# A bidirectional Mamba layer and a soft mixture of experts on one core: a second softplus kept in PSUM, a reordered prologue and epilogue, experts and merges in one block

## The reference

```python
delta = softplus(delta @ dt_proj_w.T + dt_proj_b)      # dt
dA_cum = exp(reversed cumulative sum of dt * A, shifted by one position)
xs = cumsum(dt * u * B * dA_cum) / (dA_cum + 1e-12)
y = einsum('bldn,bln->bld', xs, C) + u * D             # both directions are added, then gated
```

## Time and profile before

| what | value |
|---|---|
| runs | 6036.67, 6042.24, 6041.84 us, median 6041.84 |
| span of the profiled execution | 6039.5 us (its own time is not given apart from this; the span is 2.3 us under the median) |
| busy: PE, DVE, ACT, POOL | 5055.7 (84%), 4751.8 (79%), 4091.2 (68%), 4464.2 us (74%) |
| DMA | 755.29 MB, mean 125 GB/s |
| mean granted TensorE clock | 0.925 of full speed |

### The profile page before, as it was taken

One profiled execution on the slowest core, in us unless ns is written; L12 is line 12 of the kernel. 1 busy time (PEld: TensorE's weight loads), 2 busy tenths in 40 slices (PEclk: granted clock), 3 DMA queues, 4 the chain that ended last, 5 costly groups with the idle time before them and its releaser, 6 DMA issues. The chain is left out here.

```text
span 6039.5 us, 50725 instructions
## 1 busy us (share of the span) xinstructions
PE 5055.7 (84%) x14640; PEld 2557.8 (42%) x14640; DVE 4751.8 (79%) x4049; ACT 4091.2 (68%) x6429; POOL 4464.2 (74%) x2134
## 2 busy tenths in 40 slices
PE   5888887888887878888888888888888888999988
PEld 2333333333333333333333333443333434565566
DVE  5998989998989998999999999899999871222233
ACT  3878787878887878787878887878788863111100
POOL 3999999999999999999898999998989970000000
PEclk9999899999999999999999999999999999999988
DMA  2444344444443444444443444343434432323265
GB/s 71 129 127 132 123 129 125 130 123 128 128 132 123 129 127 126 126 126 129 124 132 124 128 127 133 126 128 124 132 124 128 130 106 83 101 76 101 80 228 203
DMA packets 555572, 755.29 MB, mean 125 GB/s; under 512 B 124059, under 2 KB 272411, under 8 KB 553245
## 3 DMA queue, kind: packets, MB, share of 16 engines
q1 hardware_dynamic: 555293, 752.04, 39.8%
HBM read 662.04 MB, written 89.82 MB: 124 GB/s over the span
## 5 line engine op out<-in xcount | busy, mean ns | idle before, releaser
L628 POOL TENSOR_TENSOR g_ring<-dtu,b_ring 128x1024 f32<-128x1024 f32 x1026 | 2514.5, 2454 | 362.2 <-DVE e_ps L976 335.1
L976 DVE TENSOR_TENSOR_SCAN e_ps<-e_ps,g_ring 128x1024 f32<-128x1024 f32 x1024 | 2345.2, 2290 | 168.3 <-ACT e_ps L782 156.2
L782 ACT ACTIVATE e_ps<-dt,a_neg 128x512 f32<-128x512 f32 x2050 | 1398.5, 682 | 721.7 <-DVE v_own L998 484.6
L1141 PE MATMUL y_ps<-v_ring,ident 128*128 128x512 f32 x3088 | 1632.2, 638 | 231.9 <-DVE res_gate L959 193.8
L637 POOL TENSOR_TENSOR v_ring<-z_ring,c_ring 128x1024 f32<-128x1024 f32 x768 | 1822.2, 2373 | 0.0
L792 ACT ACTIVATE f_ring<-rsum,consts,a_neg_half 128x512 f32<-128x512 f32 x2050 | 1645.8, 803 | 0.8
L989 DVE SCALAR_TENSOR_TENSOR z_ring<-f_ring,e_ps 128x1024 f32<-128x1024 f32 x768 | 934.9, 1217 | 49.7 <-issue 1.7
L1141 PEld LDWEIGHTS y_ps<-v_ring,ident 128*128 128x128 f32 x3088 | 592.6, 206 | 884.9 <-issue 815.3
L1141 PE MATMUL y_ps<-v_own,ident 128*128 128x512 f32 x1028 | 535.4, 616 | 0.0
L1074 PE MATMUL side<-u,conv_diag 128*128 128x512 f32 x1088 | 491.8, 595 | 23.2 <-ACT disp_ring L743 18.7
L1251 ACT ACTIVATE x_act<-x_gate,x_bg 128x512 f32<-128x512 f32 x128 | 87.9, 687 | 570.8 <-PE x_gate L1283 570.8
(11 more groups left out here) (134 smaller groups left out, 5206.1 us busy)
## 6 DMA issues: line engine op xcount, KB each, us to landing
b_ring<-bc_scr SPq DMA_DIRECT2D x1027, 256.0 KB, 3.7
c_ring<-bc_scr SPq DMA_DIRECT2D x1025, 256.0 KB, 3.4
pT_scr<-rowT_ring SPq DMA_DIRECT2D x136, 256.0 KB, 4.0
m_pT<-pT_scr SPq DMA_DIRECT2D x16, 2048.0 KB, 8.7
sT_scr<-sT_ring SPq DMA_DIRECT2D x272, 64.0 KB, 2.9
x_xT<-sT_scr SPq DMA_DIRECT2D x16, 1024.0 KB, 9.2
eo_scr<-x_eo SPq DMA_DIRECT2D x32, 512.0 KB, 5.1
m_eo<-eo_scr SPq DMA_DIRECT2D x16, 1024.0 KB, 11.0
```

What stands on the lines that cost most here:

```text
L628: pool.tensor_tensor(g_ring[:, k], dtu[d][:], both(b_ring[:, k:k + 1]), ALU.mult).then_inc(g_done, 1)
L782: act.activation(e_ps[:, i % 2, h], dt[d][:, h], ACT.Exp, scale=a_neg[:, d, c, n:n + 1]).then_inc(e_done, 1)
L976: dve.tensor_tensor_scan(e, e, g, 0.0, ALU.mult, ALU.add).then_inc(scan_done, 1)
L1141: pe.matmul(y_ps[:, t % 2], ident[:], v, start=(t % (TILES // PAIRS) < 2), stop=True, skip_group_check=True).then_inc(v_used, 1)
```

## The change

Six parts; the diff is cut to what the prediction speaks of.

1. ACT applies softplus four times: both banks to SBUF (`dt_done`), then both banks in place in PSUM (`plus_done`). DVE makes the sums with two scans of 511 elements that read the PSUM banks and a row of ones in SBUF, and these scans free the banks. POOL's `cut_chunks` now waits for the banks, and ACT's `guard` for the cut.
2. `HOLD` of dt goes from 2 to 4. By `slot_tiles` this moves the second operation of three dt pairs by one tile: dt0 3 from 36 to 37, dt1 3 from 67 to 68, dt0 1 from 98 to 99 (dt1 1 stays at 6). in0 0 stays at 38, in0 1 goes from 38 to 40, slots 2 and 3 from 68 and 71 to 70 and 72, slots 4 and 5 from 100 and 102 to 102 and 104, the operations between tiles 40 and 53 by one or two.
3. Prologue: the slots' data are loaded first and waited for alone; `v_ring` and `v_own` are cleared by POOL; the order of the side operations is that of `AHEAD`; a convolution waits only for its own diagonals; the slots' transposes go through `e_ps`; the lags of different side operations are interleaved.
4. Epilogue: the same interleaving.
5. Experts and merges share one block. Five buffers of `pT`, `x1` and `rinv` are loaded while the experts run; `eo` has two buffers, filled but for the last tile during the last expert, and that tile afterwards.
6. In the merges SP issues, once the output of sequence b-1 is computed, `pT`, `x1`, `rinv` of sequence b+4, the store of b-1, and then `eo` of b+1.

```diff
-HOLD = {..., "dt0": 2, "dt1": 2, "in0": 3,
+HOLD = {..., "dt0": 4, "dt1": 4, "in0": 3,
-AHEAD = tuple((kind, i) for kind in ("in0", "conv0", "conv1") for i in range(4)) + (
-    ("x0", 0), ("x1", 0), ("dt0", 0), ("dt0", 1))
+AHEAD = tuple((kind, i) for kind in ("in0", "conv0") for i in range(4)) + (
+    ("x0", 0), ("conv1", 0), ("dt0", 0), ("dt0", 1)) + tuple(("conv1", i) for i in range(1, 4)) + (("x1", 0),)
...
+            pool.memset(v_ring[:], 0.0).then_inc(v_cleared, 1)
+            pool.memset(v_own[:], 0.0).then_inc(v_cleared, 1)
...
             def dtu_of_pair(at, s):
+                pool.wait_ge(dt_done, at.pair(s))
...
-                pool.wait_ge(rsum_done, at.pair(s))      # cut_chunks
+                for j in (s - 1, s):
+                    pool.wait_ge(side_free[at.bank(j)], at.freed(j))
...
-                        act.activation(dt[d][:, 0], side[:, at.bank(s - 1)], ACT.Softplus).then_inc(
-                            side_free[at.bank(s - 1)], 1)
-                        act.activation(dt[d][:, 1], src, ACT.Softplus).then_inc(free, 1)
+                        both_banks = (side[:, at.bank(s - 1)], src)
+                        act.activation(dt[d][:, 0], both_banks[0], ACT.Softplus)
+                        act.activation(dt[d][:, 1], both_banks[1], ACT.Softplus).then_inc(dt_done, 1)
+                        for bank in both_banks:
+                            act.activation(bank, bank, ACT.Softplus).then_inc(plus_done, 1)
...
-                        for j in (s - 1, s):
-                            dve.wait_ge(side_free[at.bank(j)], at.freed(j))
-                        sums, steps_ = halves(rsum[d]), halves(dt[d])
...
-                        dve.tensor_tensor_scan(out, data, turn, 0.0, ALU.add, ALU.mult).then_inc(rsum_done, 1)
+                        dve.memset(rsum[d][:, :, L - 1:L] if d == 0 else rsum[d][:, :, 0:1], 0.0)
+                        for h, j in enumerate((s - 1, s)):
+                            dve.wait_ge(plus_done, 2 * at.pair(s) - 1 + h)
+                            bank, sums = side[:, at.bank(j)], rsum[d][:, h]
+                            out, data = (sums[:, 0:L - 1][:, ::-1], bank[:, 1:L][:, ::-1]) if d == 0 else (
+                                sums[:, 1:L], bank[:, 0:L - 1])
+                            dve.tensor_tensor_scan(out, data, ones[:], 0.0, ALU.add, ALU.mult).then_inc(
+                                side_free[at.bank(j)], 1)
...
-            for s in PRO:
-                for lag in range(2, 13):
-                    side_step(pro, s, lag)
+            for turn in range(len(PRO) + LAGS):
+                for k, s in enumerate(PRO):
+                    side_step(pro, s, turn - k)
...
+            def load_merge(b):
+                k = b % SLOTS
+                if b >= SLOTS:
+                    sp.wait_ge(out_done, b - SLOTS + 1)
+                sp.dma_start(pT[k][:], pT_scr[b + 1]).then_inc(p_loaded[k], 16)
...
+            for e in range(E):
+                if e + 1 < E:
+                    load(e + 1)
+                if e % 2 == 0 and e // 2 - 1 in range(SLOTS):
+                    load_merge(e // 2 - 1)
+                store(e)
+                if e == E - 2:
+                    stored_by(E - 3)
+                    for b in range(2):
+                        load_eo(b, 0, ST - 1)
+            stored_by(E - 1)
+            for b in range(2):
+                load_eo(b, ST - 1, ST)
+            for b in range(B):
+                if b >= 2:
+                    load_eo(b, 0, ST)
+                if b >= 1 and b - 1 + SLOTS < B:
+                    load_merge(b - 1 + SLOTS)
+                if b >= 1:
+                    store_out(b - 1)
```

More of the change, by code:

```diff
@@ L132, in timetable @@
     return [(name[:-1].rstrip("_"), int(name[-1])) for name in order.split()]
-HOLD = {"out": 3, "res": 4, "conv0": 4.5, "conv1": 4.5, "x0": 3, "x1": 3, "dt0": 2, "dt1": 2, "in0": 3,
+HOLD = {"out": 3, "res": 4, "conv0": 4.5, "conv1": 4.5, "x0": 3, "x1": 3, "dt0": 4, "dt1": 4, "in0": 3,
         "xnT": 2, "rows": 3, "cols": 4, "rowsT": 2, "colsT": 2, "slots": 3}
@@ L679, in _ @@
             act.activation(a_neg[:], a_neg[:], ACT.Exp).then_inc(a_exp_done, 1)
[L680 to L684 removed]
+            act.wait_ge(diag_done, 1)
             def side_step(at, s, lag):
@@ L1202, in expert_stage @@
         eo_stored = [sem(f"eo_stored{q}") for q in range(2)]
+        p_loaded = [sem(f"p_loaded{k}") for k in range(SLOTS)]
+        me_loaded = [sem(f"me_loaded{q}") for q in range(2)]
+        acc_done, y_done, chain, out_done = sem("acc_done"), sem("y_done"), sem("chain"), sem("out_done")
+        stored = [sem(f"stored{q}") for q in range(2)]
         LOADS = 7
@@ new lines, in _, with link @@
+            links = [0]
+            def link(ins):
+                links[0] += 1
+                ins.then_inc(chain, 1)
+                dve.wait_ge(chain, links[0])
+            for b in range(B):
+                q, k = b % 2, b % SLOTS
+                if b >= 1:
+                    dve.wait_ge(out_done, b)
+                dve.wait_ge(p_loaded[k], (b // SLOTS + 1) * (3 * 16))
+                for t in range(LT):
+                    dve.wait_ge(acc_done, b * LT + t + 1)
+                    dve.scalar_tensor_tensor(out=y[:, t], in0=ps[:, q * LT + t, 0:DO], scalar=rinv[k][:, t:t + 1],
+                                             in1=x1[k][:, t], op0=ALU.mult, op1=ALU.add).then_inc(y_done, 1)
+                dve.wait_ge(y_done, (b + 1) * LT)
+                if b >= 2:
+                    dve.wait_ge(stored[q], (b // 2) * 16)
+                norm_steps(dve, link, y, out_t[q], stats, mv, rstd, tmp, out_done)
@@ new lines, in _ @@
+            pe.wait_ge(eo_done, E * RT)
+            for b in range(B):
+                q, k = b % 2, b % SLOTS
+                pe.wait_ge(p_loaded[k], (b // SLOTS + 1) * (3 * 16))
+                pe.wait_ge(me_loaded[q], 32 if b < 2 else 32 + b // 2 * 16)
+                if b >= 2:
+                    pe.wait_ge(y_done, (b - 1) * LT)
+                for t in range(LT):
+                    for s in range(ST):
+                        mm = pe.matmul(ps[:, q * LT + t, 0:DO], pT[k][:, s, t * P:(t + 1) * P], me[q][:, s],
+                                       start=(s == 0), stop=(s == ST - 1))
+                    mm.then_inc(acc_done, 1)
```

365 lines of the change are left out of this document (149 added, 216 removed).

## The result

The changed kernel takes 6090.33 us in the median of four runs (6089.69 to 6090.39), the kernel before, run on the same chip, 6040.31 (6036.67 to 6042.24). The ratio is 1.0075, 95% interval 1.0054 to 1.0096: slower by 0.75%, where 5998 us was forecast.

What follows compares the result with a forecast made beforehand. DVE, with ACT right in front of it, was taken to set the loop's pace. Loop -9, prologue -13, epilogue -4, experts 0, merges -18 summed to -44 us: 6041.8 to 5998 us, 8-in-10 range 5897 to 6080.

Steps and rivals of the forecast that it cites:

- rival A: Loop: PE's clock falls to 0.50 behind new pauses at pairs 2 and 3; +4.1 us a sequence, 6071 us; chance 27%.
- pair 1: Loop, dt1 0/1, tiles stay: scan's wait of 7.5 us goes, 1.0 us of ACT is added; -6.5 us a sequence.
- pair 2: Loop, dt0 3 from tile 36 to 37: in0 0 waits for a bank DVE frees at tile 41; +1.5 us a sequence.
- pair 3: Loop, dt1 3 from tile 67 to 68: sums fall behind the scan, delaying slots 2 and `y_gate`; +6.7 us a sequence.
- pair 4: Loop, dt0 1 from tile 98 to 99: DVE's wait of 2.44 us shrinks to about 1 us; -2.3 us a sequence.
- The blocked scan: DVE's L917 sums in the loop: two scans reading PSUM never wait for POOL, 2.29 us plus a tenth against 4.17.
- ACT's second softplus: ACT at each dt pair: two more softplus cost 1.0 to 1.2 us, taken as 1.0, on DVE's path where uncovered.
- Prologue: Before the loop: slots' data first and memsets on POOL start normalisation earlier; -13 us, bounds -20 and -5.
- experts: Expert stretch: PE at 98%, no matmul removed, so nothing changes; bounds -3 and +3 us.
- merges: Final stretch: PE's first pause shrinks and the one before the last pair goes, six stay; -18 us, bounds -18 and -60.
- Epilogue: Behind the loop: interleaving cannot shorten the 24 us chain but helps the rest; -4 us, bounds -10 and +3.
- rival C: Merges without pauses, if `eo` doesn't queue behind the prefetch: -60 for -18 us, 5956 us; chance 12%.

Runs made afterwards that it cites:

- changed, pauses filled: Changed kernel with 9, 4 and 4 added zero matmuls on PE ahead of the fills of slots2, in0_0 and slots4: 6008.77 us, ratio 0.9959 to the kernel before.

## Why the prediction was wrong

The time came out by the slower rival, 6090 us for its 6071, and over the range.

**The step that failed.** The forecast worked out PE's two long pauses, of 4.8 and 9 us, and put the clock behind them at nothing; it stood only in rival A, with 27%. Measured are 4.2 and 8.1 us, a third of 4.2 us before `slots4`, and a granted clock of 0.50 behind each of them. Filling the three pauses gave back 5.2 us per sequence, and the loop then stands at -0.4 us per sequence against the kernel before, where the forecast had -0.6:

| us per sequence | forecast | changed | changed, pauses filled |
|---|---|---|---|
| pair 1 | -6.5 | -4.6 | -4.6 |
| pair 2 | +1.5 | +3.6 | +1.2 |
| pair 3 | +6.7 | +7.6 | +5.8 |
| pair 4 | -2.3 | -1.8 | -2.8 |
| sum | -0.6 | +4.8 | -0.4 |

That -0.4 comes so near to -0.6 is in part luck: pair 1 is 1.9 us too good in the forecast, and the three others, without the clock, are 1.7 us too bad together. By its own steps:

*The blocked scan.* Right: 2.4 us for a pair of scans, none blocked. The same shape takes 1206 ns from PSUM and 2968 in the mean from SBUF. With that the trace agrees with the rule of the Trainium skill ("SBUF — State Buffer", section Who interferes with whom), which the forecast weighed without a row to show it; but a scan of 2.3 us that takes 10.1 has waited for more than the one GpSimd instruction (2.4 us) that a lock of a whole instruction makes one expect.

*Pair 1.* Mis-sized: -4.6 for -6.5 us. I took the sequence of the earlier trace rows, whose scan took 9.83 us. Over the sequences it is 3.0 to 3.3 us in some and 8.3 to 10.2 in most, 7.7 in the mean. The median of 3148 ns and the mean of 4173 in the earlier trace rows left room for that.

*Pair 2.* +3.6 for +1.5 us. The forecast let PE's late `in0` reach DVE only 48 us later, at tile 58, and there it was right: DVE waits 4.62 for 3.07 us. But it had reached DVE before, at tile 42, through ACT: the scan there waits 3.97 us for an exponential that stands behind ACT's copy of `in0`. By hand that scan was to come 0.7 us earlier than pair 1 had left it; it comes 1.0 us later, and with the pauses filled 0.9 us earlier. So the forecast had the places right and lacked the slow clock, which comes in through ACT.

*Pair 3.* +7.6 for +6.7 us: mechanism and chain (scan, sums, `slots2`, adds, gate) as written. 1.4 us of it are `slots2` at the lower clock, which the forecast had left out; without the clock it is +5.8, so its size came near by two errors that partly cancel, which is luck.

*Pair 4.* -1.8 for -2.3 us. The pause of 4.2 us before `slots4` is in neither the forecast nor rival A.

So the loop's term came out at +4.8 per sequence for -0.6, 86 of the 92 us by which the time missed. Rival A had +4.1 (its own parts add up to +3.8, and 5998 + 75 is 6073 and not 6071, which changes nothing here), and its clause "2.1 us of PE's time for each pause" is near the 2.4 and 1.8 us that the filled pauses gave back at pairs 2 and 3. The earlier trace rows had shown the clock at 0.50 behind a pause of 5.23 us. With pauses of 4.8 and 9 us worked out, the forecast should have carried the clock; the one row against it, was a pause of 1.52 us.

*ACT's second softplus.* 1.09 us as reckoned; how much of it shows depends on what else pushes the same wait (3.9 us a sequence alone, 1.4 beside the holding).

*Prologue* -12.8 for -13, *experts* -1.0 for 0, *merges* -15.4 for -18, with the six pauses of 6.6 to 7.7 us where six near 6 were forecast: right. *Epilogue* -0.8 for -4: mis-sized; I didn't look for what took it back.

*Merges, rival C.* `eo` was late because SP sent it behind a prefetch and a store that wait for the norms. Asked for ahead of both, it came in time and all six pauses went. (The loads of the kernel before took up to 14.0 us to land, not 13.) Which of the two made it late, and whether the prefetch's bytes ahead of it in the queue would have held it back by themselves, as the order within one queue that the Trainium skill states ("DMA: Bandwidth & Descriptors", section Queues, rings and completion order) would have it, wasn't tried.

## What to carry to other kernels

A buffer that is freed later costs what stands behind its next writer in that engine's program order, and the length of the hold alone doesn't tell how much: look which in-order engine writes it next, what that one has queued behind, and which other in-order engine (here ACT) waits for the write ahead of work that is urgent. In this kernel PE's clock was at its lower level behind pauses of 4.2, 5.2 and 8.1 us and not behind one of 1.5 us: when an engine gains a wait of such a length, price the lower clock behind it together with the wait. And before moving work to another place, look where the engine already idles: the sums that cost 0.75% behind the scan were a gain in front of it.

## What I had not expected of the hardware

- Halving a blocked scan made it worse: 130 scans of 511 elements from SBUF take 381 us in all, where 65 of 1023 took 269; 130 from PSUM take 151 us.
- The scatter of the kernel before goes with one scan, that of pair 1: its sequences take 298 to 299 us where that scan takes 3.1 to 3.3 us and 304 to 306 where it takes 9 to 10.1, and its runs range from 5993 to 6076 us. With that scan in PSUM the runs of one kernel lie closer together: 6089.69 to 6090.39 and 5815.06 to 5819.48 us in four runs each, at most 6058.12 to 6072.50 in the seven without the second softplus. What makes the scan long in one sequence and short in the next wasn't looked for.
- Seventeen useless matmuls per sequence, in front of waits, made the kernel 1.2% faster than the same kernel without (0.9959 for 1.0075): 2.4 GHz behind the wait in place of 1.2.
